# The heads' B part with products of 64 rows, even and odd attention heads side by side in two PSUM banks, and the odd heads' rows put in place by DMA

## The reference

```python
for _ in range(2):
    logits = rms(x, norm_pre_w) @ compete_w.T + compete_b      # 16 slots
    vals, idx = top_k(swap(logits), 4); wgt = softmax(vals)
    wx = x @ write_w.T + write_b
    ws = rms(ws + einsum(wgt, wx[idx]), norm_post_w)           # (4, 16, 1024)
    q  = (x @ wq.T + bq)     # 16 heads of 64
    kk = (ws @ wk.T + bk)    # 16 slots, 16 heads of 64
    vv = (ws @ wv.T + bv)
    att = softmax(q . kk / 8)                                  # over 16 slots
    x = rms(x + (att . vv) @ out_proj_w.T + out_proj_b, norm_post_w)
return x_in + x
```

## Time and profile before

| | us |
|---|---|
| median of 3 runs | 1049.39 |
| the profiled execution, its own time | 1050.28 |
| its span on the core | 1048.5 |
| of which TensorE busy | 997.4 |
| VectorE, ScalarE, GpSimd busy | 728.0, 582.5, 431.6 |

### The profile page before, as it was taken

One profiled execution on the slowest core, in us unless ns is written; L12 is line 12 of the kernel. 1 busy time (PEld: TensorE's weight loads), 2 busy tenths in 40 slices (PEclk: granted clock), 3 DMA queues, 4 the chain that ended last, 5 costly groups with the idle time before them and its releaser, 6 DMA issues. The chain is left out here.

```text
span 1048.5 us, 15649 instructions
## 1 busy us (share of the span) xinstructions
PE 997.4 (95%) x5332; PEld 578.0 (55%) x5332; DVE 728.0 (69%) x1046; ACT 582.5 (56%) x987; POOL 431.6 (41%) x193
## 2 busy tenths in 40 slices
PE   3999999999999979999999999999799999999995
PEld 1444444444444435666666666666465666666663
DVE  6999999999999953345555555566433566666666
ACT  3888888888888721235555555566412223333332
POOL 8899999999999540000000000010200132333331
PEclk9999999999999989999999999999899999999998
DMA  4577677776775334738898888885373588888886
GB/s 165 168 233 257 220 255 243 225 252 226 252 249 178 123 105 184 243 99 284 300 300 297 288 290 293 288 275 185 121 286 140 204 295 295 293 293 303 291 293 214
DMA packets 127919, 249.11 MB, mean 238 GB/s; under 512 B 9296, under 2 KB 75472, under 8 KB 127856
## 3 DMA queue, kind: packets, MB, share of 16 engines
q1 hardware_dynamic: 127088, 246.18, 70.0%
q0 software_dynamic: 768, 2.10, 0.7%
HBM read 164.35 MB, written 83.89 MB: 237 GB/s over the span
## 5 line engine op out<-in xcount | busy, mean ns | idle before, releaser
L1083 PE MATMUL bank<-work 128*128 128x256 f32 (+1 forms) x992 | 237.0, 382 | 0.6 <-PEq L701 0.6
L1127 PE MATMUL bank<-work 128*128 128x512 f32 (+1 forms) x504 | 226.6, 592 | 0.9 <-DVE work L1186 0.9
L568 PE MATMUL bank<-work,ident 128*128 128x512 f32 x384 | 188.6, 614 | 20.3 <-DVE work L463 19.0
L1083 PEld LDWEIGHTS bank<-work 128*128 128x128 f32 x992 | 181.3, 190 | 35.4 <-issue 16.2
L1386 POOL TENSOR_TENSOR work<-work 128x1024 f32<-128x1024 f32 x30 | 70.8, 2359 | 206.2 <-DVE work L1228 206.2
L1127 PEld LDWEIGHTS bank<-work 128*128 128x128 f32 x504 | 95.7, 190 | 94.7 <-issue 90.4
L1161 DVE TENSOR_TENSOR work<-bank,sbias 128x256 f32<-128x256 f32 x64 | 27.2, 425 | 152.5 <-PE bank L1083 143.5
L568 PEld LDWEIGHTS bank<-work,ident 128*128 128x128 f32 x384 | 66.0, 191 | 106.0 <-issue 78.4
L568 PE MATMUL bank<-work 128*128 128x511 f32 x256 | 121.4, 598 | 0.0
L326 POOL DMA_INDIRECT work<-x_natural_scratch,gidx x16 | 14.7, 921 | 245.6 <-DVE gidx L300 241.9
L455 DVE SCALAR_TENSOR_TENSOR work<-work,decay 128x512 f32<-128x512 f32 x128 | 98.8, 830 | 0.0
(11 more groups left out here) (164 smaller groups left out, 1411.5 us busy)
## 6 DMA issues: line engine op xcount, KB each, us to landing
x_natural_scratch<-work SPq DMA_DIRECT2D x64, 512.0 KB, 5.1
work<-x_natural_scratch SPq DMA_DIRECT2D x64, 512.0 KB, 4.8
work<-in_kT SPq DMA_DIRECT2D x32, 512.0 KB, 3.8
work<-in_xT SPq DMA_DIRECT2D x32, 512.0 KB, 3.9
x0T_scratch<-work SPq DMA_DIRECT2D x32, 512.0 KB, 3.3
work<-x0T_scratch SPq DMA_DIRECT2D x32, 512.0 KB, 6.4
x1T_scratch<-work SPq DMA_DIRECT2D x32, 512.0 KB, 3.0
work<-x1T_scratch SPq DMA_DIRECT2D x32, 512.0 KB, 6.0
```

The source lines that it names most:

```text
L568: return nc.tensor.matmul(ps[:, at:at + n], w, v, start=start, stop=not start, skip_group_check=True)
L1083: last = nc.tensor.matmul(ps_s[p], xTb[p][:, c, :], Amat[:, i, :, c * 32:c * 32 + 32], start=(c == 0), stop=(c == NC - 1))
L1127: last = nc.tensor.matmul(ps_o[:, cols], attT[:, k * P:(k + 1) * P], Bmat[k][:, i, cols], start=(k == 0), stop=(k == 1), skip_group_check= ...
```

## The change

The groups become 4, one for each half k of the pairs and each two batches r. `vvz` is held as (128 rows, 8 pairs, 2, 2 batches, 16 slots): no zeros and no memset of it. A product takes 64 rows (one attention head, e = 0 even or e = 1 odd), 32 columns (16 slots of two batches) and 512 columns of `wo`; even heads write one PSUM bank, odd heads another, and there are again 64 products per head of the program. The even bank holds, in each strip of 32 partitions, rows of batch 2r in the lower 16 and of batch 2r+1 in the upper 16; the odd bank has the two batches the other way round. For batch 2r+1 the order of the two heads in a pair is swapped, in `kkz` as well, so that rows stay in their partitions. The engines copy the whole even bank to both batches (first and second), and the odd bank to `Bodd`, in the place of `wq`. Then DMAs copy the odd heads' 16 rows of each strip from `Bodd` to `Bmat`: `send_rows` issues 4 DMAs of 16 rows x 4 KB, and is called 8 times per round, twice at the end of the head and six times in the tail's steps 0, 1 and 2. The 24 early weight loads move from steps 4..27 to 8..27, two of them in each of the last four steps.

```diff
-        vvz = cut(44160, 1024).rearrange("p (h b s) -> p h b s", h=HP, b=B)
+        vvz = cut(44160, 512).rearrange("p (h r b s) -> p h r b s", h=HP, r=2, b=2)
-        groups = [(k, b) for b in range(B) for k in range(2)]
+        groups = [(k, r) for r in range(2) for k in range(2)]
+        Bodd = [cut(1024 * g, C) for g in range(4)]
+        def send_rows(sp, t, g, e):
+            k, r = groups[g]
+            sp.wait_ge(grp_odd[k], 2 * t + r + 1)
+            sp.wait_ge((grp_first if e else grp_second)[k], 2 * t + r + 1)
+            for j in range(4):
+                rows = slice(32 * j + S * e, 32 * j + S * e + S)
+                sp.dma_start(Bmat[k][rows, 2 * r + 1 - e, :], Bodd[g][rows, :]).then_inc(brows_in[r][e], 16)
...
-                return banks[1 + g % 3]
+                return banks[(1, 2, 3, 0)[2 * (g % 2) + e]]
...
+                    for g in range(2):                    # SP, end of the head
+                        send_rows(sp, t, g, 1)
...
-                        if g == 2:
+                        if g == 1:
+                            wait_product(pe, HP - 2)
                             wait_product(pe, HP - 1)
-                        wait_group(pe, g - 3)
+                        if g > 1:
+                            pe.wait_ge(grp_odd[k], 2 * t + r)
+                            pe.wait_ge(grp_first[k], 2 * t + r)
+                            pe.wait_ge(grp_second[k], 2 * t + r)
...
+                                for e in range(2):
+                                    rows = slice(64 * e, 64 * e + 64)
+                                    last = nc.tensor.matmul(group_bank(g, e)[32 * j:32 * j + 32, cols],
+                                                            vvz[rows, 4 * k + j, r, :, :], weights["wo"][1][4 * k + j][rows, cols],
...
+                    pe.wait_ge(grp_odd[1], 2 * t + 2)
                     pe.wait_ge(xT_in[0], 16 + 256 * t)
...
-                    nc.gpsimd.memset(vvz.rearrange("p h b s -> p (h b s)"), 0.0).then_inc(kz, 1)
...
+                        if k == 0:
+                            act.wait_ge(grp_first[k], 2 * t + r + 1)
+                            nc.scalar.activation(Bmat[k][:, 2 * r + 1, :], group_bank(g, 0)[:, :], ACT.Copy).then_inc(grp_second[k], 1)
+                        else:
+                            nc.scalar.activation(Bodd[g], group_bank(g, 1)[:, :], ACT.Copy).then_inc(grp_odd[k], 1)
+                            act.wait_ge(grp_second[k], 2 * t + r + 1)
+                            nc.scalar.activation(Bmat[k][:, 2 * r, :], group_bank(g, 0)[:, :], ACT.Copy).then_inc(grp_first[k], 1)
...
+                        if k == 0:
+                            nc.vector.tensor_tensor(Bmat[k][:, 2 * r, :], group_bank(g, 0)[:, :], obias[:], ALU.add).then_inc(grp_first[k], 1)
+                            nc.vector.tensor_tensor(Bodd[g], group_bank(g, 1)[:, :], obias[:], ALU.add).then_inc(grp_odd[k], 1)
+                        else:
+                            nc.vector.tensor_copy(Bmat[k][:, 2 * r + 1, :], group_bank(g, 0)[:, :]).then_inc(grp_second[k], 1)
...
+                        if isinstance(m, int) and m < 3:       # SP, step(m), behind load_x
+                            for k in range(2):
+                                send_rows(sp, t, (0, 2, 2)[m] + k, (0, 1, 0)[m])
...
+                            if isinstance(m, int) and m == 0:  # TensorE, before the output product
+                                pe.wait_ge(brows_in[0][1], 128 * t + 128)
+                            if isinstance(m, int) and m == 3:
+                                pe.wait_ge(brows_in[0][0], 128 * t + 128)
+                                for e in range(2):
+                                    pe.wait_ge(brows_in[1][e], 128 * t + 128)
```

More of the change, by code:

```diff
@@ L629, in build @@
         Bmat = [BM[:, 4096 * k:4096 * k + 4096].rearrange("p (b x) -> p b x", b=B) for k in range(2)]
-        groups = [(k, b) for b in range(B) for k in range(2)]
+        groups = [(k, r) for r in range(2) for k in range(2)]
+        Bodd = [cut(1024 * g, C) for g in range(4)]
+        brows_in = [[sem(f"B_rows_in_{r}_{e}") for e in range(2)] for r in range(2)]
+        def send_rows(sp, t, g, e):
[5 more added lines that the diff above has]
+                sp.dma_start(Bmat[k][rows, 2 * r + 1 - e, :], Bodd[g][rows, :]).then_inc(brows_in[r][e], 16)
+        grp_odd, grp_first, grp_second = ([sem(f"B_{v}_{k}") for k in range(2)] for v in ("odd", "first", "second"))
         sbias = sb("sbias", [P, B, HS])
@@ L665, in head @@
             prod_ps, ev_a, ev_d, sb_ps, sb_ok = (hsem(x) for x in ("prod_ps", "ev_act", "ev_dve", "sb_ps", "sb"))
-            grp_ps, grp_d, grp_a, ob_zero, ob_in = (hsem(x) for x in ("B_ps", "B_dve", "B_act", "bias_zero", "bias_in"))
+            grp_ps, ob_zero, ob_in = (hsem(x) for x in ("B_ps", "bias_zero", "bias_in"))
             psW, psK, psV = banks[0][:, 0:512], banks[0][:, 512:1024], banks[1][:, 0:512]
@@ L685, in wait_product, with group_bank @@
                     eng.wait_ge(ev_d if i % 2 else ev_a, i // 2 + 1)
[L687 to L694 removed]
+            def group_bank(g, e):
+                return banks[(1, 2, 3, 0)[2 * (g % 2) + e]]
             def keep_warm(n):
@@ L816, in _ @@
                     pe.wait_ge(sb_ok, 1)
-                    for g, (k, b) in enumerate(groups):
+                    for g, (k, r) in enumerate(groups):
                         if g < 2:
@@ L820, in _ @@
                                 wait_weights(pe, "wo", 4 * k + j)
-                        if g == 2:
+                        if g == 1:
+                            wait_product(pe, HP - 2)
                             wait_product(pe, HP - 1)
-                        wait_group(pe, g - 3)
-                        for h in range(2):
-                            cols = slice(CH * h, CH * h + CH)
-                            for j in range(4):
[L827 to L833, removed]
+                        if g > 1:
+                            pe.wait_ge(grp_odd[k], 2 * t + r)
+                            pe.wait_ge(grp_first[k], 2 * t + r)
+                            pe.wait_ge(grp_second[k], 2 * t + r)
+                        for half in range(2):
+                            cols = slice(CH * half, CH * half + CH)
+                            for j in range(4):
+                                for e in range(2):
+                                    rows = slice(64 * e, 64 * e + 64)
+                                    last = nc.tensor.matmul(group_bank(g, e)[32 * j:32 * j + 32, cols],
+                                                            vvz[rows, 4 * k + j, r, :, :], weights["wo"][1][4 * k + j][rows, cols],
+                                                            start=True, stop=True, skip_group_check=True)
+                            last.then_inc(grp_ps, 1)
+                    pe.wait_ge(grp_odd[1], 2 * t + 2)
                     pe.wait_ge(xT_in[0], 16 + 256 * t)
@@ L884, in _ @@
                         copy_product(act, lambda o, x: nc.scalar.activation(o, x, ACT.Copy), i)
[L885 to L888, removed]
+                    for g, (k, r) in enumerate(groups):
+                        act.wait_ge(grp_ps, 2 * g + 2)
+                        if k == 0:
[5 more added lines that the diff above has]
+                            nc.scalar.activation(Bmat[k][:, 2 * r, :], group_bank(g, 0)[:, :], ACT.Copy).then_inc(grp_first[k], 1)
                 @block.vector
@@ L938, in _ @@
                         sum_rows(dve, t, 1, k)
-                    dve.wait_ge(kz, 2)
+                    dve.wait_ge(kz, 1)
                     spread(0, 0, kkz, bkc, kt_ps, kk_ok)
@@ L949, in _ @@
                     dve.wait_ge(ob_in, 16)
[L950 to L954, removed]
+                    for g, (k, r) in enumerate(groups):
+                        dve.wait_ge(grp_ps, 2 * g + 2)
+                        if k == 0:
+                            nc.vector.tensor_tensor(Bmat[k][:, 2 * r, :], group_bank(g, 0)[:, :], obias[:], ALU.add).then_inc(grp_first[k], 1)
+                            nc.vector.tensor_tensor(Bodd[g], group_bank(g, 1)[:, :], obias[:], ALU.add).then_inc(grp_odd[k], 1)
+                        else:
+                            nc.vector.tensor_copy(Bmat[k][:, 2 * r + 1, :], group_bank(g, 0)[:, :]).then_inc(grp_second[k], 1)
         x1s = [cut(38912 + 1024 * i, 1024) for i in (0, 1)]
@@ L1055, in step @@
                             load_residual(m - 2, p)
-                        if first and 4 <= m < 28:
+                        if isinstance(m, int) and m < 3:
+                            for k in range(2):
+                                send_rows(sp, t, (0, 2, 2)[m] + k, (0, 1, 0)[m])
+                        if first and m == 8:
+                            for r in range(2):
+                                for e in range(2):
+                                    sp.wait_ge(brows_in[r][e], 8 * 16)
+                        if first and 8 <= m < 28:
```

(8 more changed lines are left out.)

12 lines of the change are left out of this document (9 added, 3 removed).

## The result

The changed kernel takes 1058.13 us (median of 4 runs, 1057.9 to 1058.37) where the kernel before, on the same chip, takes 1049.55 (4 runs, 1049.15 to 1049.77). The ratio is 1.0088 (95% interval 1.0076 to 1.01): 8.6 us slower. The forecast was 1047.6, with a range to 1054.5: size and sign were wrong.

A forecast was written before the change was run, and what follows sets the result against it. TensorE, busy 95% of the span, was taken as the bound. Heads -7.7 us and tails +5.9 us sum to -1.8 us, giving 1047.6 us against a median of 1049.39, range 1043.5 to 1054.5.

The forecast's parts named there:

- The products: In each head, B's 64 products run eight side by side and take 6.93 us in place of 13.87.
- rival 5: In the heads, the array's two row halves take turns, so products save nothing: 1057.7 us, chance 0.12.
- The copies and waits in the head: Waits for copies out of PSUM take 3.1 of 6.93 us saved per head, leaving 3.86; both heads -7.7 us.
- The row copies in the tail: Sixteen copies on SP ahead of tile 2's load halt TensorE 3.0 and 2.1 us; with slow issues, +5.9 us together.
- Issue: In the tail, SP issues one row copy in 0.46 us, so 16 ahead of tile 2's load take 7.5 us.
- Landing: Tile 2's load of x lands 4.1 us after issue in the first tail, 3.2 us in the second.
- The allowance of 0.4 per tail for slow issues: An occasional slow DMA issue on SP, 1.0 us over its neighbours, was counted as 0.4 us per tail.
- The clock: TensorE's clock was assumed to stay at 1.00 through the halts before tile 2's scores, adding nothing to the sum.
- rival 3: TensorE's clock falls to 0.50 in the first tail's halt, adding 3.4 us: 1051.0 us, chance 0.15.
- rival 4: Row copies queue in the tails and push the load back 2.9 us per tail: 1053.4 us, chance 0.12.
- The edits counted as nothing: Memset of vvz, early weight loads, the head's row copies and tile 3's load in the tail: 0 us each.
- The second rival: In the tails, a 16-row issue takes half of 0.46 us, so tile 2's load lands in time: 1041.7 us, chance 0.1.

The follow-up runs named there:

- half copies: Changed kernel with tail row copies in steps 2, 3, 4 directly behind loads of x, and each head group's first copy per bank cut into two column halves: 1039.8 us.
- the first variant: Changed kernel with the tail's 24 row copies moved from steps 0, 1, 2 to steps 2, 3, 4, behind each step's load of x: 1046.93 us, ratio 0.9971.
- the variant without halts: Changed kernel with the tail's row copies in steps 2, 3, 4, directly behind the load of x and ahead of the store: 1040.81 us, ratio 0.9927.

## Why the prediction was wrong

**The products, right.** Two groups (32 products, 64 records) take 3.66 us to the last one's end, where 32 products before took 6.9 (13.87 / 2). The halves of the array work side by side; rival 5 (turns) is false, which is as the Trainium skill, page "TensorEngine Tiling (Array Packing)", section "Tiling Modes", has it.

**The copies and waits in the head, right.** Forecast 3.86 us saved in each head; the rows show 3.91 and 3.63. Gaps forecast as 1.1 and 0.6, measured 0.95 and 0.20, and 1.25 before the scores. That the first head agrees to 0.05 us is partly luck: the waits are 2.4 us for the 3.1 forecast, and the rest of B's 9.96 us is 7.6 for 6.93. The half copies confirm the cause.

**The row copies in the tail: the step that failed.** The sum had +5.9 us for both tails; the rows show 12.7, and 4.4 for the clock. Its terms:

- *Issue, mis-sized*: 0.46 us came from a DMA out of DRAM, and I moved it to a copy within SBUF without a bound above. It is 0.63. Over 16 issues that is 2.7 us per tail, 5.4 in all, which would alone have turned the sum from -1.8 to +3.6.
- *Landing, mis-sized in the first tail*: 4.1 us was a load with nothing behind it for five us. With the changed order eight copies stand behind it, and it took 6.0: 1.9 us. In the second tail 3.5 for 3.2.
- The allowance of 0.4 per tail for slow issues stands for nothing that the trace shows.
- *The clock* was taken at 1.00 in the sum, with the fall as rival 3 (3.4 us in the first tail, chance 0.15). It fell in both halts, 1.6 and 2.8 us. The argument against it ("the halt is shorter" than the 4.78 us of the earlier trace rows) did not hold even for the forecast halt of 3.0 us: the first variant's halt of 2.88 us brought the fall too. And the trace of before has more than the one stretch at 0.50 that the prediction read: one more lies at the end of the first tail, amid short gaps, of which none in the 20 us ahead of it is over 1.61 us:

```profile
744.30:751.10 6.80, 5.25 (x29) 2.79 (x33) 3.24 (x5) 2.28 (x5) 0.83 (x1) 0.50 0.25 94
```

**The queue of row copies (rival 4), false in its mechanism though its sign came.** In the first tail the halt was over 5 us and the load landed more than 5 us behind its issue, as this rival had it. But the copies land 2.3 to 2.5 us behind their issue, the first as the last: nothing piles up. While little else moved, the DMA engines were busy for 0.65 of the time:

```profile
447.00:456.00 9.00, 6.82 (x24) 3.87 (x22) 5.09 (x12) 1.72 (x4) 0.95 (x1) 1.00 0.65 102
```

That is an estimate of 0.41 us of their time per copy (0.65 x 0.63), between the prediction's ends of 0.16 and 0.64 and under the time of an issue. The Trainium skill's section "Door 1: The DMA port swizzle" (page "SBUF — State Buffer") gave an estimate of 0.60 us per copy; an issue every 0.63 us is longer than that too, so these copies make no queue by it either, and no run here measures the rate itself. The nearest forecast by number is rival 5's, 1057.7 for 1058.13; that is chance, as its mechanism is false.

**The edits counted as nothing** (memset, weight loads, the head's row copies, tile 3's load): no idle time in the traces points at one, and the variant without halts is 8.8 us faster than the kernel before. The second rival, "the late load hardly counts", names 1041.7: that is the price that the same change has with its copies in another place.

## What to carry to other kernels

Count the issues that a change puts ahead of a load on an in-order queue, price them by an issue of the same kind (source and target), and compare the sum with the load's slack: here 16 x 0.63 + 6.0 us against 8.6. A halt can cost twice, since the clock can fall in it: here it did in all of 2.9 us and more. Copies that nothing reads soon belong behind the load of the next tile, and the wait for them at the first tile that reads them; then look for what they now make late, since here each move showed the next one.

## What the runs showed of the hardware

- SP issues a DMA within SBUF every 0.63 us, for 16 rows x 1 KB as for 32 rows x 4 KB or 128 rows x 1 KB, and one from DRAM every 0.46.
- A load of 512 KB at the same place of the first tail landed in 4.1 us with nothing issued behind it for five us (two traces), and in 4.6 to 6.2 us with eight copies of 64 KB directly behind it (seven traces), whether or not 16 such copies stood ahead.
- The clock fell to 0.50 inside tail halts of 7.4, 7.1, 5.8, 5.0, 4.6 and 2.9 us, each time amid dense work, and stood there for 6.83 us; it stayed at 1.00 through gaps of 1.46 and 1.69 us. At the end of the first tail it fell amid short gaps, none over 1.61 us.
